# Self-attention in four row strips, and both attentions in one program per engine

## The reference

```python
# self-attention: 16 query heads of 16, ONE key head and ONE value head, causal
q = (hidden_states @ q_w.T + q_b).reshape(b, s, H, HEAD_DIM)
k = hidden_states @ k_w.T + k_b
v = hidden_states @ v_w.T + v_b
scores = jnp.einsum('bqhd,bkd->bhqk', q, k) / HEAD_DIM ** 0.5
scores = jnp.where(causal[None, None], -jnp.inf, scores)
attn = jax.nn.softmax(scores.astype(jnp.float32), axis=-1)
out = jnp.einsum('bhqk,bkd->bqhd', attn, v).reshape(b, s, H * HEAD_DIM)
return out @ o_w.T + o_b
# cross-attention: 32 heads of 8, q and k turned by a rotary position code
logits = jnp.einsum('bqhd,bkhd->bhqk', q, k) * scale
w = jax.nn.softmax(logits, axis=-1)
# whole block
x = x + _L0_attn_ref(_layernorm(x, axis=-1), ...)
x = x + _L0_xattn_ref(_layernorm(x, axis=-1), ctx_1024, ...)
x = x + _L0_ffn_ref(_layernorm(x, axis=-1), ...)
```

## Time and profile before

| | us |
|---|---|
| median of 3 runs | 840.25 (835.55 to 841.25) |
| the profiled execution, its own time | 842.49 |
| its span in the trace | 840.7 |
| PE busy in the span | 706.3 (84%) |
| DVE, POOL, ACT busy | 449.6, 391.9, 302.8 |
| mean granted TensorE clock, as a share of 2.4 GHz | 0.908 |

### The profile page before, as it was taken

The page is one execution under the profiler, slowest core; times in us unless marked ns, Lnnn a source line. Parts: engine busy times, 40 slices in busy tenths (PEclk is TensorE's granted clock), DMA queues, the critical chain, the costliest instruction groups (busy, mean ns, idle before and its releaser), DMA issues. The chain is left out here.

```text
span 840.7 us, 17941 instructions
## 1 busy us (share of the span) xinstructions
PE 706.3 (84%) x6319; PEld 550.8 (66%) x6319; DVE 449.6 (53%) x1023; ACT 302.8 (36%) x675; POOL 391.9 (47%) x496
## 2 busy tenths in 40 slices
PE   3877787887368999999987588948999999999985
PEld 2855666664257888878875256835777777777774
DVE  5376665663334466656551788973222222222798
ACT  0324343443102444454452363312333333333431
POOL 3346554563422122122200475354777777776653
PEclk9969999999655799999996699987999999999998
DMA  6111111110011111111100598001333333332941
GB/s 178 38 39 41 33 37 30 39 46 16 7 31 26 26 27 30 34 34 28 27 16 2 179 235 204 1 26 57 101 101 105 104 103 105 101 102 88 308 162 37
DMA packets 60803, 61.01 MB, mean 73 GB/s; under 512 B 8194, under 2 KB 55028, under 8 KB 60724
## 3 DMA queue, kind: packets, MB, share of 16 engines
q1 hardware_dynamic: 52436, 38.42, 17.3%
q0 software_dynamic: 7584, 20.72, 7.6%
q10 hardware_dynamic: 704, 0.79, 0.3%
HBM read 34.34 MB, written 14.55 MB: 58 GB/s over the span
## 5 line engine op out<-in xcount | busy, mean ns | idle before, releaser
L1585 PE MATMUL s<-wx,routed_out 128*128 x316 | 109.2, 469 | 1.1 <-ACT routed_out L1288 1.1
L1456 DVE TENSOR_TENSOR routed_out<-s,routed_out 128x176 f32<-128x176 f32 x79 | 27.0, 341 | 142.0 <-ACT routed_out L1293 142.0
L1220 POOL DMA_INDIRECT slot_rows<-stage,dest x79 | 78.2, 990 | 35.2 <-issue 19.8
L843 ACT ACTIVATE b_pt<-s 128x1024 f32<-128x1024 f32 x64 | 63.5, 1020 | 81.1 <-PE s L895 81.1
L1186 POOL DMA_INDIRECT routed_in<-normed_rows,token x79 | 77.9, 986 | 31.0 <-issue 19.7
L1604 PE MATMUL last<-wx,routed_out 88*128 x316 | 81.5, 380 | 0.7 <-DVE routed_out L1461 0.6
L824 DVE TENSOR_REDUCE b_mx<-s 128x8 f32<-128x1024 f32 x32 | 39.2, 1224 | 79.2 <-PE s L934 79.2
L439 DVE TENSOR_REDUCE mx<-s 128x4 f32<-128x512 f32 x64 | 43.9, 686 | 57.7 <-PE s L570 57.0
L1585 PEld LDWEIGHTS s<-wx,routed_out 128*128 128x128 f32 x316 | 54.8, 193 | 19.1 <-issue 2.5
L782 POOL TENSOR_TENSOR b_rot<-b_by_cos,b_by_sin 128x256 f32<-128x256 f32 x16 | 12.4, 775 | 99.3 <-DVE b_by_cos L811 91.2
L1604 PEld LDWEIGHTS last<-wx,routed_out 88*128 88x128 f32 x316 | 53.7, 190 | 5.7 <-issue 1.4
(11 more groups left out here) (273 smaller groups left out, 1700.9 us busy)
## 6 DMA issues: line engine op xcount, KB each, us to landing
wx<-slot_rows SPq DMA_DIRECT2D x16, 512.0 KB, 9.1
qs<-qhi SPq DMA_DIRECT2D x64, 64.0 KB, 2.5
b_qk<-b_rot SPq DMA_DIRECT2D x128, 32.0 KB
wx<-in_w_gate SPq DMA_DIRECT2D x4, 528.0 KB
wx<-in_w_up SPq DMA_DIRECT2D x4, 528.0 KB
wx<-in_w_down SPq DMA_DIRECT2D x4, 528.0 KB
x_sb<-in_x SPq DMA_DIRECT2D x4, 512.0 KB, 7.1
qs<-qlo SPq DMA_DIRECT2D x32, 64.0 KB, 2.5
```

Of the source, the lines that this page charges most:

```text
L843: nc.scalar.activation(pt[:, c % 2, u].rearrange("p h q -> p (h q)"), s2[:, u].rearrange("p a n -> p (a n)"), ACT.Exp, scale=HD_B ** -0.5) ...
L1220: nc.gpsimd.indirect_dma_start(out=slot_rows[:, :], out_offset=bass.IndirectOffsetOnAxis(ap=dest[:, n:n + 1].bitcast(U32), axis=0), in_=ys ...
L1585: last = nc.tensor.matmul(s2[:, n % 2, 0, 0:2 * FE], xT[:, n % 2, P * k:P * k + P], wx[:, bass.ds(e, 1), 2 * FE * k:2 * FE * k + 2 * FE].r ...
```

## The change

Self-attention is written anew in the manner of cross-attention. q and k stay plain float32: no split on POOL, no L473 on DVE. The keys' projection weights are repeated in four strips, so that one projection gives k in each strip with a row of ones behind it. `scores` is four masks into four banks and 16 multiplications of 16 contraction rows, 128 columns each (L494 of the changed kernel); `shifted` is four multiplications of 17 contraction rows and 512 columns, one in each strip (L457). Four DMAs instead of six bring q into place (L333). The row maximum is two DVE instructions of 1,024 elements instead of four of 512 (L358, L359). Steps run from -7 to 17, all written out. The turned x, the turned output, the output projection and the projections have separate places in PSUM.

A new function `attention` makes one block of both pipelines: at step t every engine runs the self step t (up to 17) and behind it the cross step t - 19 (from -8 on). So cross steps -8 to -2 stand in self steps 11 to 17, and the first cross `shifted` is at t = 19. The tiles of cross-attention are cleared at the start of the block and at t = -4. `mixture` is unchanged.

```diff
+    def sync(sp, c):
+        b = c + 1
+        if there(b):
+            sp.wait_ge(mT_out, b + 1)
+            sp.dma_start(qa[HD_A:P:32, b % SL], mT[:, b % 2, :]).then_inc(mrow_in[b % 2], 16)
+        b = c + 4
+        if there(b):
+            sp.wait_ge(qkv_out, b + 1)
+            for i in range(4):
+                sp.dma_start(qa[32 * i:32 * i + HD_A, b % SL, 2:4, :], qa[32 * i + HD_A:32 * i + 32, b % SL, 0:2, :]).then_inc(stack_in[b % SL], 16)
...
+    def vector(dve, c):
+        h = c + 2
+        if there(h):
+            need(dve, mT_done, h - 1)
+            dve.wait_ge(s1_done, h + 1)
+            nc.vector.tensor_reduce(mx[:, h % 2, 0:8], s2[:, 0].rearrange("p a (n k) -> p (a n) k", n=4), AX.X, ALU.max).then_inc(max_done, 1)
+            nc.vector.tensor_reduce(mx[:, h % 2, 8:16], s1[:].rearrange("p a (n k) -> p (a n) k", n=4), AX.X, ALU.max).then_inc(max_done, 1)
+        b = c - 2
+        if there(b):
+            dve.wait_ge(out_done, b + 1)
+            dve.wait_ge(ob_added, b + 1)
+            nc.vector.tensor_tensor(x[:, b, :], s2[:, 1, 1, D:2 * D], x[:, b, :], ALU.add).then_inc(x_added, 1)
...
+            dve.wait_ge(rstd_done, b + 1)
+            need(dve, trx_done, b - 1)
+            nc.vector.tensor_scalar(xn[:, b % 2, :], x[:, b, :], mv[:, b % 2, 0:1], rstd[:, b % 2, 1:2],
+                                    ALU.subtract, ALU.mult).then_inc(xn_done, 1)
...
+        exps(c, 0)
+        b = c + 1
+        if there(b):
+            act.wait_ge(mT_done, b + 1)
+            if b >= 2:
+                act.wait_ge(mrow_in[b % 2], 16 * (b // 2))
+            nc.scalar.copy(mT[:, b % 2, :], s1[0:UH, 0, 0:P]).then_inc(mT_out, 1)
...
+        exps(c, 1)
+        b = c - 1
+        if there(b):
+            act.wait_ge(pv_done, b + 1)
+            need(act, tb_done, b)
+            nc.scalar.copy(sums[:], acc[:]).then_inc(sums_out, 1)
...
+        b = c + 4
+        if there(b):
+            act.wait_ge(proj_done, b + 1)
+            need(act, s2_done, b - SL + 1)
+            need(act, pv_done, b - VS + 1)
+            if b == 0:
+                act.wait_ge(init, 1)
+            for k in range(KC):
+                nc.scalar.activation(qa[:, b % SL, k, :], mid[:, P * k:P * k + P], ACT.Identity, bias=g["qkb"][:, k:k + 1])
+            nc.scalar.activation(ka[:, b % SL, :], mid[:, 2 * P:3 * P], ACT.Identity, bias=g["qkb"][:, 2:3])
+            nc.scalar.copy(v[:, b % VS, 0:HD_A], mid[:, 3 * P:3 * P + HD_A]).then_inc(qkv_out, 1)
...
+    def tensor(pe, c):
+        def shifted(b):
+
+            if not there(b):
+                return
+            pe.wait_ge(mrow_in[b % 2], 16 * (b // 2 + 1))
+            pe.wait_ge(max_done, 2 * upto(b + 1) - 1)
+            need(pe, exp_done, 2 * b)
+            pe.wait_ge(xnT_done, upto(b + 4))
+            need(pe, oT_done, b - 2)
+            need(pe, x_added, b - 2)
+            need(pe, g["cross"]["xcT_done"], crossed(b))
+            if b == 0:
+                pe.wait_ge(tab_out, 8)
+            for i in range(4):
+                rows = slice(32 * i, 32 * i + HD_A + 1)
+                last = nc.tensor.matmul(second_bank(i), ka[rows, b % SL, :], qa[rows, b % SL], start=True, stop=True)
+            last.then_inc(s2_done, 1)
+
+        def turn_max(b):
+
+            if not there(b):
+                return
+            pe.wait_ge(max_done, 2 * b + 2)
+            nc.tensor.matmul(s1[:, 0, 0:P], mx[:, b % 2, :], g["nident"][:], start=True, stop=True).then_inc(mT_done, 1)
...
+        def values(b):
+
+            if not there(b):
...
+            pe.wait_ge(causal_done, 2 * b + 2)
+            need(pe, o_normed, b)
+            for half in range(2):
+                for n in range(4):
+                    last = nc.tensor.matmul(acc[VW * n:VW * n + VW, 2 * P * half:2 * P * half + 2 * P], v[:, b % VS, :],
+                                            pt[:, b % 2, n // 2, 4 * (n % 2) + 2 * half:4 * (n % 2) + 2 * half + 2, :], start=True, stop=True)
+            last.then_inc(pv_done, 1)
+
...
+            pe.wait_ge(stack_in[b % SL], 16 * 4 * (b // SL + 1))
+            if there(c):
+                pe.wait_ge(exp_done, 2 * c + 1)
+            for i in range(4):
+                if i == 2:
+                    need(pe, max_done, 2 * b)
+                    need(pe, mT_out, b)
+                nc.tensor.matmul(first_bank(i), g["identb"][:], g["mask_q"][:], start=True, stop=False)
+            for n in range(4):
+                for i in range(4):
+                    rows = slice(32 * i, 32 * i + HD_A)
+                    last = nc.tensor.matmul(first_bank(i)[:, P * n:P * n + P], qa[rows, b % SL, n, :], ka[rows, b % SL, :], start=False, stop=(n == 3))
+            last.then_inc(s1_done, 1)
...
+        shifted(c)
+        turn_max(c + 1)
+        values(c - 1)
+        scores(c + 2, c)
+        b = c - 2
+        if there(b):
+            pe.wait_ge(o_normed, b + 1)
+            if there(c):
...
+                last = nc.tensor.transpose(s2[:, 1, 1, P * k:P * k + P], o[:, b % 2, P * k:P * k + P], g["ident"][:])
+            last.then_inc(trO_done, 1)
+        b = c + 5
+        if there(b):
+            pe.wait_ge(xn_done, b + 1)
+            if there(c):
+                pe.wait_ge(exp_done, 2 * c + 2)
+            need(pe, xnT_done, b)
+            for k in range(KC):
...
+            last.then_inc(trx_done, 1)
...
+        b = c - 1
+        if there(b):
+            pe.wait_ge(sums_out, b + 1)
+            for i in range(4):
+                last = nc.tensor.transpose(acc[:, P * i:P * i + P], sums[:, P * i:P * i + P], g["ident"][:])
+            last.then_inc(tb_done, 1)
+        b = c - 2
+        if there(b):
+            pe.wait_ge(oT_done, b + 1)
+            for k in range(KC):
+                last = nc.tensor.matmul(s2[:, 1, 1, D:2 * D], oT[:, b % 2, k, :], g["woT"][:, k, :], start=(k == 0), stop=(k == KC - 1))
+            last.then_inc(out_done, 1)
+        b = c + 4
+        if there(b):
...
+            pe.wait_ge(xnT_done, b + 1)
+            need(pe, qkv_out, b)
+            for m in range(2):
...
+    def vector(dve, c):
+        b = batch(c - 4)
+        if b is not None:
+            dve.wait_ge(out_done, b + 1)
+            dve.wait_ge(ob_added, b + 1)
+            nc.vector.tensor_tensor(x[:, b, :], mid[:, 0:D], x[:, b, :], ALU.add).then_inc(x_added, 1)
+        b = batch(c + 8)
+        if b is not None:
+            dve.wait_ge(before["x_added"], b + 1)
+            nc.vector.bn_stats(stats[:, b % 2, :], x[:, b, :]).then_inc(ln_stats, 1)
...
+            if not half(h):
+                return
+            if h == 0:
+                pe.wait_ge(before["x_added"], NB)
+            pe.wait_ge(mrow_in[(h // 2) % 2], 16 * (h // 4 + 1))
...
+        def scores(h, c):
+
+            if not half(h):
+                return
+            b, u = h // 2, h % 2
+            if u == 0:
+                pe.wait_ge(qk_in[b % SL], STACK * (b // SL + 1))
+            if h == 0:
+                pe.wait_ge(before["exp_done"], 2 * NB)
+                pe.wait_ge(before["max_done"], 2 * NB)
+                pe.wait_ge(before["mT_out"], NB)
...
+        b = batch(c + 6)
+        if b is not None:
+            pe.wait_ge(xcT_done, b + 1)
+            need(pe, x_added, (c - 4) // 2 + 1)
+            if b == 0:
+                pe.wait_ge(before["qkv_out"], NB)
...
+def attention(nc, io, g, tmp):
+
+    own = self_attention(nc, g, tmp)
+    a = g["self"]
+    other = cross_attention(nc, io, g, a, tmp)
+    b = g["cross"]
+    first, last = a["steps"][0], b["steps"][1] + BEHIND
+
+    def step(eng, n, t):
+
+        if t <= a["steps"][1]:
+            own[n](eng, t)
+        if t - BEHIND >= b["steps"][0]:
+            other[n](eng, t - BEHIND)
...
+            for t in range(first, last + 1):
+                if t - BEHIND == b["steps"][0]:
+                    sp.wait_ge(b["init"], 3)
+                step(sp, 0, t)
...
+            for t in range(first, last + 1):
+                if t == 1 - 5:
+                    nc.gpsimd.memset(b["qk"][:, 2:4], 1.0).then_inc(b["init"], 1)
```

More of the change, by code:

```diff
@@ L68, in need, with by_strip @@
     eng.wait_ge(sem, value)
-def valid(j, c, n):
-    return not isinstance(j, int) or 0 <= 4 * j + c < n
-def cap(value, most):
-    return min(value, most) if isinstance(value, int) else value
-def steps(eng, step, first, enter, looped, last):
-    for c in range(first, enter):
-        step(0, c)
-    with eng.Fori(0, looped) as j:
-        for c in range(enter, enter + 4):
-            step(j, c)
-    for c in range(enter + 4 * looped, last + 1):
-        step(0, c)
-def by_pair(row):
-    return row.rearrange("p (q d u g) -> p u q g d", q=2, d=HD_A, u=2)
+def by_strip(row):
+    return row.rearrange("p (k i y d) -> p y k i d", k=2, i=4, y=2)
 def prepare(nc, io, g, tmp):
@@ L837, in _ @@
+            nc.vector.memset(a["mx"][:], 0.0)
+            nc.vector.memset(b["mx"][:], 0.0)
+            for t in range(first, last + 1):
```

(11 more changed lines are left out.)

928 lines of the change are left out of this document (354 added, 574 removed).

## The result

The changed kernel takes 800.6 us in the median of four executions (795.1 to 806.1), the kernel before 839.6 on the same chip; the ratio is 0.954 (95% interval 0.946 to 0.963). A second series on another chip gave 799.2 (794.8 to 801.5) and 0.951 (0.944 to 0.958). An execution that took over 1.5% longer than the fastest of its kernel, at a lower granted clock, is left out of the ratios (1057.2 of e1_no_overlap, 803.8 and 806.8 of e4_filler, 789.3 of e7_behind18, one of the kernel before in each of two series). So the change is worth about 40 us. The forecast was 770 with a range of 756 to 793: the direction was right, the size was not, and the time lies outside the range. In the profiled executions the gain is 842.5 - 797.5 = 45.0 against 69.9 in the sum.

A forecast was written before the change was run, and what follows sets the result against it. It took self-attention as bound by a chain through PE, DVE and one PSUM bank, and the stretch between blocks by idleness and low clock. Gains 6.3 + 54.0 + 9.6 = 69.9 from 842.5 gave 772.6, median 770, range 756 to 793.

The forecast's parts named there:

- signs of being wrong: Stated beforehand: a step near 10, `shifted` over 2 us, or a clock of 0.50 in the middle of the attentions.
- The step: Steady self-attention: PE's row of work sets each step, 8.6 us, with no wait for x_sb.
- The rival chain: Self-attention: a path over ACT, SP and the maximum row makes the step 10.0, total 787; chance 0.12.
- the serial strips: Self `shifted`: strips of 512 columns do not run side by side, 4.24 instead of 1.10, total 820; chance 0.05.
- (A): Filling before self-attention: first self `shifted` starts at 51 instead of 57.3, a gain of 6.3 us.
- (B): From first self to first cross `shifted`: 143.9 us instead of 197.9, a gain of 54.0.
- 10.5 against 9.9: Cross fill: 10.5 us left for batch 0's q and k rows, which took 9.9 from POOL's product to `scores`.
- (C): First cross batches: full clock instead of the slow one, a gain of 9.6 us.
- the fill does not fill: Cross fill: batch 0's rows late, PE idles in steps 16 to 18, some 20 us lost, total 800; chance 0.04.

The follow-up runs named there:

- e1_no_overlap: Changed kernel with BEHIND 26 instead of 19, so cross steps begin only behind the last self step: 813.2 us, ratio 0.963.
- e4_filler: Changed kernel with extra matmuls nobody reads (four in step 12, five in step 14) ahead of PE's waits for normalized cross rows: 801.9 us, ratio 0.945.
- e7_behind18: e6_order with the cross pipeline one step earlier (18 steps behind instead of 19): 782.4 us, ratio 0.928.
- e2_late_clear: Changed kernel with POOL's and DVE's clearing of b_qk moved from the filling to self steps 3 and 4: 789.9 us, ratio 0.938.
- e6_order: Changed kernel with clearing in self steps 3 and 4, early Exp table, and cross normalization, rotation and transposes put ahead of self work: 774.0 us, ratio 0.921.
- e10_keep_busier: e6_order plus unread matmuls ahead of PE's waits, six in the cross fill and five in steps 14 to 16: 768.2 us, ratio 0.918.

## Why the prediction was wrong, point by point

Two of its own signs of being wrong came: `shifted` over 2 us (2.09), and a clock near 0.50 in the middle of the attentions (0.52 from 168.8).

**The step (right, and better).** 8.6 was forecast and 8.21 measured, without a wait for x_sb: 3.5 us more gain in steps 2 to 10. Most of the 0.38 lies in the eight transposes (0.93 for 1.12) and the output projection (0.94 for 1.06). The strips run side by side with 512 columns too: from start to start 1.07, against the 1.10 of rows 6. The estimate by the Trainium skill's rule (TensorE: Matmul & The Clock Gate, Part 3) was 1.38; this row does not bear it out. The rival chain (10.0) and the serial strips did not come.

**(A), the filling: the term that failed first.** 51 was forecast, 61.0 measured. "The clearing, for which I take half a batch, 3.4": it cost 7.5 (e2_late_clear), 4.1 more. 3.4 is about the length of one of the two clearings (3.51 and 3.47); the other had no term, although DVE stands still while POOL clears and then clears itself. With the clearing moved away the block starts at 53.5, where the sum without its 3.4 gives 47.6: the other 5.9 lie in the filling itself. For them there are two candidates in e2_late_clear, which its trace does not separate: the clock, 0.52 from 35.0 to 48.6 where the sum had it full, and PE's waits of 2.90 and 3.27 for transfers and copies, which had no term.

**(B), 155.4 for 143.9.** Steps 0 and 1 took 8.9 and 7.1 for 6.6 and 7.3; step 0 holds the table load and a slow stretch, and without both it took 6.5 (e6_order). Steps 12 to 15 took 9.7, 10.7, 9.3 and 8.4, together 38.1, for 7.0, 8.0, 5.2 and 6.9, together 27.1. That 11.0 is the step of the sum that failed most: "step 12 8.6 - 0.3 - 1.8 + 0.5" counts the PE work that drops out and comes in, and no wait. The new waits (1.86 + 0.66, 2.66 + 0.66) follow from the order of DVE's list, which the order of the code shows, and they bring two slow stretches with them. The prediction looked at whether the rotated rows of batch 0 come in time (10.5 against 9.9; they do, the first cross scores wait for nothing) and not at the normalized rows one stage before, nor at batch 1, whose rotated rows were 3.07 late: from scores to `shifted` 16.0 for 13.8. With the list reordered the same stages took 28.7 for steps 12 to 15 (e6_order: 8.1, 7.9, 6.2, 6.6) and 10.9.

**(C), 9.9 for 9.6, but for other reasons.** "PE now has no stretch without work of more than 3 us ahead of it": it had one (3.07), and the clock did fall, at 212.5. But the 3 us had no row behind them, and the trace of before speaks against them as a limit. There the clock fell within 0.5 us of PE's stop at 217.6, behind waits of 0.3 to 0.8 us in the last steps of self-attention, and it fell within self-attention too, behind waits for x_sb (0.94 on the mean in rows 1 hides that):

```profile
93.71 0.41 PE L608 MATMUL last<-ident,xn 128*128 128x128 f32 x2 [3.24 <-DVE x_sb L484]
...
105.08 0.45 PE L608 MATMUL last<-ident,xn 128*128 128x128 f32 x2 [1.82 <-DVE x_sb L484]
```

```profile
95.30:98.30 3.00, 3.00 (x19) 2.47 (x12) 0.68 (x3) 0.59 (x1) 0.00 (x0) 0.50 0.00 0
105.50:108.50 3.00, 3.00 (x21) 1.41 (x20) 1.43 (x4) 0.56 (x2) 0.73 (x2) 0.50 0.20 51
218.00:218.50 0.50, 0.00 (x0) 0.00 (x0) 0.09 (x2) 0.00 (x0) 0.16 (x1) 0.50 0.00 0
```

So a wait of 1.82 within a step was followed by the lower level, and one of 1.75 (rows 3, at 180.55) was not. So the trace of before already showed that a wait within a step can cost clock as well; the sum looked only for stretches without work. The first two cross batches still lose 3.2 us (27.4 against 24.2) and gain 6.4 on before; the other 3.5 come from the end of attention, which before ran at the lower level from 446.9 on, up to its end and beyond (30.7 us in all), and now in two shorter stretches. The amount is right by luck.

**The mixture, 3.7 us with no term.** It was taken as unchanged. It is unchanged in its work; but in the profile of after the clock is 0.55 from 441.8 to 448.6, in the shared expert's first products, and again from 766.0 to 772.9, where before it was full. Windows of after and then of before, of 12 us at the same place of the program:

```profile
440.00:452.00 12.00, 11.34 (x36) 7.44 (x37) 8.86 (x61) 6.46 (x14) 5.78 (x7) 0.72 1.05 277
```

```profile
488.70:500.70 12.00, 10.85 (x44) 7.30 (x44) 9.63 (x58) 8.07 (x16) 8.39 (x9) 1.00 1.09 283
```

36 against 44 multiplications in the 12 us: the first twelve of them with `early_hi` and `early_lo` take 4.90 us after and 2.90 before, so 2.0 us are lost there. In the eleven experiments it took between 374.4 (e10_keep_busier) and 379.5 (e1_no_overlap); it moves with the clock, not with its own code.

**The rivals.** The one that came nearest, "the fill does not fill" at 800, had 0.04. Its time is right, and its mechanism partly: cross rows come late and PE idles. But it put them in steps 16 to 18 and had all of (C) lost with 20 us of (B); it was 11.5 of (B), none of (C), and 10 of (A). The chance was too small because the sum had tested one transfer for lateness and called the fill by that.

## What to carry to other kernels

When a second pipeline is laid behind a first in each engine's list, PE's work is the smallest part of the price: for each producer of the new work, see what stands ahead of it in that producer's own list, and put the new work at the head of the step, where the engine idles; here that (with the Exp table, and with what the clock gave) was worth 16 us (e2_late_clear to e6_order), more than the 13 of the overlap itself. Clearings and other one-time work belong where an engine idles in the steady steps and not in the filling, and DVE's copies and a clearing on POOL are not to be counted as side by side. Where a forecast needs the full clock in a stretch with gaps, its range should carry both levels; and gaps that can't be closed may be filled with matmuls that nobody reads (6 us less here, about 3 of them in the attentions).

## What the runs showed of the hardware

- A POOL memset of 3.51 us held up a row of eight float32 copies of DVE for 3.4 us; with it gone they took 1.70 and not 5.07.
- Four strips of 17 rows and 512 columns in float32 take 1.07 us together from start to start, as long as one of 512 columns over all rows would by rows 6 (twice 0.53).
- PE idle for 2.5 to 3.3 us within a step is followed by 6.4 to 6.8 us at 1.2 GHz, and with matmuls in the gap it is not (one profile). Behind waits of 0.5 to 1.1 us scattered over steps 14 to 16 it fell at 191 (e6_order) and 183 (e9_keep_busy); with them filled it fell first at 205 (e10_keep_busier). In the kernel before, a wait of 1.82 us (105.08) was followed by 0.50, one of 1.75 (180.55) was not. A stretch of 30.7 us at 0.51 with PE busy 30.7 of 30.7 us (e4_filler, 229.3) is not explained by these runs.
- Executions of one program differed by 11 us (795.1 to 806.1) and, e4_filler's, by 15.6 (791.3 at a mean clock of 0.935, 806.8 at 0.918), those of e2_late_clear only by 0.6.
